# Second attention on one Trainium2 core: distance products in two 64-column tiles, and trips of 92 of the 128 query rows

## The reference

```python
q = _heads(x @ Wq); k = _heads(ctx_t @ Wk); v = _heads(ctx_t @ Wv)
sim = jnp.einsum('bihd,bjhd->bhij', q, k) * SCALE
dist = jnp.clip(jnp.arange(TEXT)[None, :] - jnp.arange(nq)[:, None], -MAXREL, MAXREL) + MAXREL
k2 = rel_k[dist]
sim = sim + jnp.einsum('bihd,ijd->bhij', q, k2) * SCALE
attn = jax.nn.softmax(sim, axis=-1)
out = jnp.einsum('bhij,bjhd->bihd', attn, v)
out = out + jnp.einsum('bhij,ijd->bihd', attn, rel_v[dist])
out = out + stream(Wk_ip, Wv_ip, ctx_i) * (jnp.tanh(alpha) + 1.0)
out = out + stream(Wk_ap, Wv_ap, ctx_a) * (jnp.tanh(beta) + 1.0)
return out.reshape(b, nq, INNER) @ Wo + bo
```

## Time and profile before

| | |
|---|---|
| time, median of 3 runs | 996.27 us (995.89 to 1000.37) |
| span of the profiled execution | 992.7 us, 3.6 us under the median |
| TensorE busy | 891.3 us, 90% of the span |
| VectorE, ScalarE, GpSimd busy | 612.0, 469.1, 379.8 us |
| DMA | 222059 packets, 137.78 MB, 160289 of the packets under 512 bytes |
| layer 0 and experts | about 0 to 450 us |
| attention 1, before its first `prob_out` | about 450 to 559 us |
| loop of attention 1 | about 559 to 866 us |
| feed-forward part | about 866 to 993 us |

### The profile page before, as it was taken

The page is one execution under the profiler, slowest core; times in us unless marked ns, Lnnn a source line. Parts: engine busy times, 40 slices in busy tenths (PEclk is TensorE's granted clock), DMA queues, the critical chain, the costliest instruction groups (busy, mean ns, idle before and its releaser), DMA issues. The chain is left out here.

```text
span 992.7 us, 26217 instructions
## 1 busy us (share of the span) xinstructions
PE 891.3 (90%) x8784; PEld 758.1 (76%) x8785; DVE 612.0 (62%) x1561; ACT 469.1 (47%) x1209; POOL 379.8 (38%) x555
## 2 busy tenths in 40 slices
PE   4888889777999999997999899999999999779995
PEld 3677667636999999995556598888888887667784
DVE  3588788754455555542017466768667686549895
ACT  3777777712222222221333444445444454349895
POOL 4477677530000000006101446445464444426762
PEclk9998999987999999998999999999999999879998
DMA  4454447432433333315765798897989986411121
GB/s 119 145 164 145 143 148 237 140 145 94 128 108 93 98 93 108 93 44 181 262 225 180 165 188 185 179 182 164 200 172 176 172 178 150 90 33 55 60 61 49
DMA packets 222059, 137.78 MB, mean 139 GB/s; under 512 B 160289, under 2 KB 207393, under 8 KB 221857
## 3 DMA queue, kind: packets, MB, share of 16 engines
q1 hardware_dynamic: 180304, 99.78, 40.1%
q10 hardware_dynamic: 38608, 28.64, 10.8%
q0 software_dynamic: 3072, 8.39, 2.6%
HBM read 81.79 MB, written 54.98 MB: 138 GB/s over the span
## 5 line engine op out<-in xcount | busy, mean ns | idle before, releaser
L1717 ACT ACTIVATE c_pT<-c_T 128x512 f32<-128x512 f32 (+2 forms) x90 | 50.2, 595 | 104.4 <-PE c_T L1876 73.3
L1666 POOL TENSOR_TENSOR c_soft<-c_soft,c_share 128x616 f32<-128x616 f32 (+2 forms) x96 | 70.3, 760 | 63.4 <-DVE c_share L2129 61.8
L1062 ACT ACTIVATE b_rowsT<-b_RT 128x256 f32<-128x256 f32 x39 | 15.0, 383 | 158.2 <-PE b_RT L1104 158.2
L1173 DVE COPY b_w<-moe_w 128x1024 f32 x78 | 53.5, 687 | 56.2 <-issue 50.7
L1676 POOL MEMSET d_round<- 128x1 f32 x1 | 0.1, 98 | 226.5 <-POOLq L953 226.5
L1113 PEld LDWEIGHTS b_G<-b_rowsT,b_w 128*128 128x128 f32 x624 | 77.2, 195 | 4.2 <-DVE b_w L1173 1.5
L1113 PE MATMUL b_G<-b_rowsT,b_w 128*128 128x128 f32 x624 | 77.9, 279 | 1.5 <-ACT b_rowsT L1062 1.3
L1113 PE MATMUL b_U<-b_rowsT,b_w 128*128 128x128 f32 x624 | 76.1, 275 | 0.0
L1187 DVE SCALAR_TENSOR_TENSOR b_hidT<-b_U,b_bias,b_gate 128x128 f32<-128x128 f32 x156 | 43.9, 343 | 51.9 <-PE b_U L1113 45.4
L1140 PE MATMUL b_Y<-moe_w,b_hidT 128*128 x312 | 73.9, 380 | 0.9 <-DVE b_out L1218 0.9
L1113 PEld LDWEIGHTS b_U<-b_rowsT,b_w 128*128 128x128 f32 x624 | 72.9, 192 | 0.0
(11 more groups left out here) (231 smaller groups left out, 2167.2 us busy)
## 6 DMA issues: line engine op xcount, KB each, us to landing
rel_windows<-c_relw ACTq DMA_DIRECT2D x28, 368.0 KB, 6.7
c_bias<-rel_windows SPq DMA_DIRECT2D x16, 616.0 KB, 5.6
prob_rows<-c_soft SPq DMA_DIRECT2D x16, 616.0 KB, 7.3
moe_w<-in_L_Wl SPq DMA_DIRECT2D x16, 512.0 KB, 4.1
early<-in_L_early SPq DMA_DIRECT2D x16, 384.0 KB, 3.2
values<-c_pT ACTq DMA_DIRECT2D x22, 256.0 KB, 3.8
b_rows<-expert_lists SPq DMA_DIRECT2D x39, 128.0 KB, 2.0
expert_out<-b_out SPq DMA_DIRECT2D x39, 128.0 KB, 1.7
```

The lines of the kernel that those rows point to most:

```text
L1173: nc.vector.tensor_copy(own[p][h][:, :, :], w1[:, bass.ds(e, 1), :, h * HE:(h + 1) * HE].rearrange("p o c n -> p (o c) n"))\
L1666: ins = nc.gpsimd.tensor_tensor(soft[p][:, hs, a:z], soft[p][:, hs, a:z], share[:, s, hs].unsqueeze(2).to_broadcast([P, HS, z - a]), ALU.mult)
L1717: nc.scalar.activation(dst, view(T[k]), ACT.Copy, **kw).then_inc(g["emptied"], 1)
```

## The change

1. `distances`: each of the 16 products becomes two, for the two halves of its weights, put at array columns 0 and 64 with `tile_position`. There are 32 products, each with 128 x 64 weights and 64 columns streaming.
2. `rel_in`, `prob_out`, `band_in` and the transfer in `windows` take rows 0 to 91 (`NEAR`) in place of 0 to 127. Runs a row and bytes a run stay.
3. `band_values` streams 92 columns in place of 128.
4. GpSimd sets all of both `band` tiles to zero once, then waits until the text values are through (`filled`), and sets all of both `bias` tiles to zero. SP waits for these four before the first `rel_in`.

```diff
+NEAR = TEXT + MAXREL - 1
...
+        s_far = sem("c_far_rows")
...
-                sp.dma_start(bias[p][:, :, :], sheared(rel_d[p], P - 1, -1, P, TEXT)).then_inc(s_relin[p], 16)
+                sp.dma_start(bias[p][0:NEAR, :, :], sheared(rel_d[p], P - 1, -1, NEAR, TEXT)).then_inc(s_relin[p], 16)
...
-                sp.dma_start(prob_d[p][:, :, MAXREL:MAXREL + TEXT], soft[p][:, :, 0:TEXT]).then_inc(s_pout[p], 16)
+                sp.dma_start(prob_d[p][0:NEAR, :, MAXREL:MAXREL + TEXT], soft[p][0:NEAR, :, 0:TEXT]).then_inc(s_pout[p], 16)
...
-                sp.dma_start(band[p][:, :, 0:NSTEP - 1], sheared(prob_d[p], 1, 1, P, NSTEP - 1)).then_inc(s_pin[p], 16)
+                sp.dma_start(band[p][0:NEAR, :, 0:NSTEP - 1], sheared(prob_d[p], 1, 1, NEAR, NSTEP - 1)).then_inc(s_pin[p], 16)
...
+            sp.wait_ge(s_far, 4)
             for q in two:
                 rel_in(q, 0, q)
...
+            for p in two:
+                nc.gpsimd.memset(band[p][:, :, :], 0.0).then_inc(s_far, 1)
+            pool.wait_ge(g["filled"], 2 * MT1 + 2 * (TEXT_TILES - EARLY_TILES))
+            for p in two:
+                nc.gpsimd.memset(bias[p][:, :, :], 0.0).then_inc(s_far, 1)
             pool.wait_ge(s_folded, 1)
...
-                    act.dma_start(rel_d[p][:, h * HS:(h + 1) * HS, at:RELW], w[:, :, at:RELW]).then_inc(s_relout[h], 16)
+                    act.dma_start(rel_d[p][0:NEAR, h * HS:(h + 1) * HS, at:RELW], w[0:NEAR, :, at:RELW]).then_inc(s_relout[h], 16)
...
-                    for j in range(MS):
-                        ins = nc.tensor.matmul(bank[:, j * 2 * NSTEP:(j + 1) * 2 * NSTEP], qT[p][:, u * MS + j, :], relk[:, :],
-                                               start=True, stop=True)
+                    for j, a in itertools.product(range(MS), two):
+                        half = slice(a * DH1, (a + 1) * DH1)
+                        ins = nc.tensor.matmul(bank[half, j * 2 * NSTEP:(j + 1) * 2 * NSTEP], qT[p][:, u * MS + j, half], relk[:, :],
+                                               start=True, stop=True, tile_position=(0, a * DH1))
...
-                            ins = nc.tensor.matmul(O[u][a * DH1:(a + 1) * DH1, q, :], steps_v[r, :], bandT[r, q, :],
+                            ins = nc.tensor.matmul(O[u][a * DH1:(a + 1) * DH1, q, 0:NEAR], steps_v[r, :], bandT[r, q, 0:NEAR],
                                                    start=False, stop=(q == BT - 1), tile_position=(r.start, a * DH1))
```

## The result

The changed kernel takes 1181.39 us (median of 4 runs, 1178.72 to 1182.24), before 996.62 us beside it. The ratio is 1.185, with a 95% interval of 1.182 to 1.188. The prediction was 1270 us, with a range of 1180 to 1370: slower as forecast, but only 1 us inside the low end of the range. The range of the forecast case by itself, 1204 to 1354, doesn't hold it. The loss is 185 us, where 274 was worked out.

A forecast was written before the change was run, and what follows sets the result against it. TensorE was taken to bound the loop (95% busy), with DMA engines almost full. Steps growing from 20.16 to 38 us gave +250, the loop's end +16, before it +8: 1270 us, range 1180 to 1370.

The forecast's parts named there:

- Four engines: All four trips: 92 rows run on four engines, 23 rows each, not 16 with 8; forecast case, chance 0.76.
- the loss of transfers that run together: Loop step: kinds running together are slower, factor 1.3; 31.6 us of work without it, 41 with all, 35.5 taken.
- other transfers on the busiest engine: Loop step: values, keys, x, x3, context and picked rows add 4.5 us on the busiest engine.
- the gap behind `prob_out`: Loop step: SP's queue is empty from the last packet of `prob_out` to the first of `band_in`, 2.5 us.
- The path: Loop: TensorE's 20 us no longer cover the trips at 38 us a step; TensorE waits for `band_in`; +250 us.
- Ends: Before the loop, whole windows and `rel_in(0)` on four engines: +8 us (0 to 15); after the fifteenth `prob_out`: +16.
- Zeroing: Four GpSimd memsets before the first `rel_in`, 3.3 us in all, covered by idle time: nothing.
- Distances: TensorE in the loop: 32 products for 16 cost about 0, bounds +1.7 and -0.9 us a step.
- the switches of the array's shape: TensorE tiling: changed distances add no switch beyond the one the band values already make; the sum would not move.
- All engines share: Rival: 92 rows use all sixteen engines, TensorE stays the bound, 990 us (975 to 1020); chance 0.08.
- Well overlapped: Rival: four engines with two queues overlapping well, 29 us a step, 1135 us; chance 0.08.
- one after another: Rival: four engines, windows and SP's trips not overlapping, 47 us a step, 1400 us; chance 0.08.

The follow-up runs named there:

- the probabilities' trips alone: Changed kernel with windows and `rel_in` back at 128 rows, only `prob_out` and `band_in` at 92: 1051.32 us.
- the bias trips alone: Changed kernel with `prob_out` and `band_in` back at 128 rows, only windows and `rel_in` at 92: 1078.28 us.
- three engines: Changed kernel with 93 rows in place of 92 in all four trips and the band values: 1328.94 us, ratio 1.338.
- the kernel with the products alone: Kernel before with only the new `distances` (32 products) and `band_values` (92 columns), all trips at 128 rows: 987.29 us, ratio 0.994.

## Why the prediction was right, and where its sizes were off

**Four engines.** Right, and shown: 92, 93, 96 and 100 rows are four counts within 9% of each other and give 31.8, 41.2, 19.7 and 19.8 us a step. The shares of 23, 31, 6 and 10 rows on the busiest engine order them; neither the bytes nor the multiples of 4 do. The reading of the earlier trace rows, 11.3 engines for 77 rows, was enough for it. The rate of a trip shows it directly. The last `prob_out` runs nearly alone, and the table by stretch inside it reads, at 92, 93, 100 and 96 rows:

```profile
1040.00:1042.00 2.00, 1.67 (x4) 1.40 (x5) 0.00 (x0) 0.28 (x1) 0.00 (x0) 0.50 0.32 58
...
1186.00:1188.00 2.00, 2.00 (x6) 1.55 (x6) 0.00 (x0) 0.00 (x0) 0.00 (x0) 0.50 0.24 44
...
859.00:860.00 1.00, 1.00 (x5) 0.86 (x4) 0.00 (x0) 0.00 (x0) 0.62 (x2) 0.71 0.75 158
...
849.00:850.00 1.00, 1.00 (x4) 0.82 (x3) 0.00 (x0) 0.00 (x0) 0.82 (x2) 0.50 1.02 236
```

44, 58, 158 and 236 GB/s, divided by 3, 4, 10 and 16 engines, are 14.7, 14.5, 15.8 and 14.8 GB/s an engine; at 128 rows it was 261 GB/s, 16.3 an engine. The ratio of 261 to 58 is 4.5, a little over 16/4. The DMA share reads higher than the count of engines (0.32, where four of sixteen are 0.25), for a reason that no run shows, so the engines are counted by the rate.

**The size.** The step was put at 38 us and is 31.8, under the 34 that was its low end. That the time still lies in the stated range is owed to the room which that range left for the rivals. The terms:

```profile
889.00:890.00 1.00, 1.00 (x23) 0.88 (x24) 0.00 (x0) 0.84 (x2) 1.00 (x2) 0.50 0.30 75
...
1032.00:1034.00 2.00, 0.00 (x0) 0.00 (x0) 1.36 (x4) 0.00 (x0) 1.88 (x4) 0.50 0.34 52
```

The first of these is inside a `rel_in`, the second inside a `band_in` of the changed kernel. So `prob_out` takes 453 KB / 58 = 7.8 us (6.9 predicted), `rel_in` 453/75 = 6.0 (7.5), `band_in` 183/52 = 3.5 (4.9). The windows are never alone, but their step back to 16 engines gave 4.9 us, so they take 2.7 + 4.9 = 7.6 (7.8). Sum 24.9 us, 27.1 predicted: 2.2 us too many, from rates that were read at sixteen engines and for `rel_in` and `band_in` were low there.

The larger miss, 3.9 us, is the loss of transfers that run together. It was read from the earlier trace rows, where two kinds on sixteen engines get 200 GB/s in place of 261 to 279, and about two fifths of it was carried over. On four engines no such loss shows. Behind the issue of a windows transfer and of a `prob_out` the table reads:

```profile
893.08 2.45 ACTq L1785 DMA_DIRECT2D rel_windows<-c_relw  x1
...
893.17 0.77 SPq L1561 DMA_DIRECT2D prob_rows<-c_soft  x1
...
899.00:901.00 2.00, 1.53 (x25) 1.28 (x24) 1.60 (x4) 0.75 (x2) 0.26 (x2) 1.00 0.34 58
```

That is 58 GB/s, as for the lone `prob_out`. No row has the windows alone on four engines, so a small loss isn't excluded. Where the loss comes from on sixteen engines wasn't tested; that it is gone when four are at work fits a limit that all engines share, not one inside each.

The rest, other transfers on the busiest engine and the gap behind `prob_out`, was put at 4.5 + 2.5 = 7.0 us. What is left for it is 31.8 - 24.9 = 6.9; no row measures it by itself. With this one number fitted the other runs follow within 0.7 us: the probabilities' trips alone 11.3 + 5.3 + 6.9 = 23.5 (measured 23.3), the bias trips alone 13.6 + 4.1 + 6.9 = 24.6 (25.0), windows at 128 rows 26.9 by construction, three engines 24.9 x 31/23 + 6.9 = 40.5 (41.2). So a step is the busiest engine's work and the gap, with nothing hidden by a second queue. The sum over the loop was mis-sized by 14 x 6.2 = 87 of the 89 us by which the prediction missed.

**The path.** Right that the cover of 20 us is gone and that TensorE waits for the band, 74.0 us. Incomplete in two points: TensorE waits almost as long for the keys (64.4 us), and VectorE waits 47.1 us for the bias. All three come through SP's queue and the four busy engines; that they are one and the same delay is argued from this order, not tested by itself. One sign was off: TensorE's share in the loop, forecast near half, is 0.67 (317.8 of 477 us), since the step is shorter than forecast and the busy time grew at a granted clock of 0.80.

**Ends.** Before the loop +13.7 us (8 predicted, within 0 to 15). It comes from the first windows' trips: with windows at 128 rows the first `prob_out` is at 557.0 and 558.7 us, with windows at 92 at 573.0 and 573.6. Behind it +10.1 (16 predicted).

**Zeroing.** Nothing that shows, as predicted: the kernel with 96 rows contains it.

**Distances.** Wrong in size, hidden by the rest. "About 0" was taken by the values' products, with 128 columns streaming; the distances stream 64. The low bound, -0.9 us, was nearly right: -0.83. Of that and the band values' -0.24, half a microsecond a step shows (two products: 19.65 us a step, before 20.16). In the changed kernel even that doesn't show, since TensorE waits anyhow. It also often runs at the lower clock (1.2 GHz) after its waits: the same 32 distances took 1.90 us at 887.85, in a stretch with a granted clock of 0.55.

```profile
887.85 1.90 PE L1947 MATMUL c_T<-c_steps_k,c_qT 128*64 128x64 f32 x32
...
887.80:889.60 1.80, 1.80 (x34) 1.71 (x32) 0.60 (x2) 1.18 (x3) 1.68 (x3) 0.55 0.30 75
```

The prediction also counted the switches of the array's shape wrongly. The queries ahead of the distances are 128*128 products, the distances are now 128*64 and the band values 32*64, so there is one switch more than before, not none. It costs nothing that shows: the idle time before the distances is 0.25 us before and in the kernel with the products alone.

**Rivals.** All engines share: fell, but it is what happens at 96 rows, and its 990 us is near the 986 measured there. Well overlapped (29 us a step) and one after another (47) both fell; the truth lies between the first and the forecast, but not for the first's reason.

## What to carry to other kernels

Before a transfer is made smaller by rows, factor the new row count: what counted in all these runs is the largest divisor up to 16, so 96 is a cheap 92, and 93 a ruinous one. When a trip gets slower while the DMA share falls, ask how many engines it runs on, since the share is a mean over sixteen. And a trip on few engines wasn't paid here by its own latency, which slack may cover, but by its work on the busiest engine, which was added to that of all others.

## What the runs showed of the hardware beyond this

The attention's trips on fewer than sixteen engines have no time to landing in the page, in every run here: 92, 93 and 100 rows lack it, 96 and 128 rows have it. In the experiments of mixed rows just the 92-row trips lack it. So a trip that loses the number when its rows change is worth a look. It is a hint and no proof, since transfers that nothing changed can lack it too: `moe_w` of 512 KB has 4.1 us before, and no number in the changed kernel and in the one with 96 rows.

The Trainium skill, page "DMA: Bandwidth & Descriptors", section "Why a DMA increments its semaphore by 16 and not by 1", would explain it for the trips: with k engines only k increments come from data. The runs show the gap in the rows, not the increments.

SP itself can be held at an issue. In the changed kernel, right behind a `prob_out` and with the windows under way, up to the `band_in`:

```profile
893.17 0.77 SPq L1561 DMA_DIRECT2D prob_rows<-c_soft  x1
894.21 15.75 SPq L1571 DMA_DIRECT2D rows_after_attention<-c_x  x1
913.12 0.28 SPq L1567 DMA_DIRECT2D c_band<-prob_rows  x1
```

The store of 128 rows took 15.75 us to issue, where it took 2 to 3 before. What limits it wasn't tested. It delays what SP issues next, if that isn't waiting for something else: `band_in` comes 3.2 us behind the end of this issue, after a wait for the `prob_out` to land.
